# One row-by-row column in three groups instead of one in six: SyncE's share of the gather in a graph network's last edge pass

## The chip, the cores and the metric

One core of a Trainium2 chip runs the whole program in one launch. The metric is the device time of one execution in microseconds (us); the number compared is the median of several executions. The profile is one execution taken by the hardware profiler, with its own span.

The engines are called PE (TensorE), DVE (VectorE), ACT (ScalarE), POOL (GpSimd) and SP (SyncE). SP computes nothing: it waits, branches, loads registers and issues DMAs.

## The reference, cut to what matters

The reference is four graph layers on 12,500 nodes and 200,000 edges, sorted by destination. The change touches the last one, whose node features `h` have 64 floats:

```python
def _L3_gnn_ref(h, ef, gamma, beta, src, dst):
    z = h[src] + h[dst] + ef
    deg = segment_sum(ones, dst); deg_safe = maximum(deg, 1.0)[:, None]
    mean    = segment_sum(z, dst) / deg_safe
    mean_sq = segment_sum(z * z, dst) / deg_safe
    std = sqrt(relu(mean_sq - mean * mean) + EPS_STD)
    mx, mn = segment_max(z, dst), segment_min(z, dst)
    agg = concatenate([mean, mx, mn, std], axis=1)
    ...                        # degree scalers, mean over 13 parts, batch norm over the nodes
```

The edge pass computes, for every edge, the running sum and running maximum over its destination's edges of `h[src] + ef`, of its square and of its negative. The gather `h[src]`, one row of 256 bytes for each of the 200,000 edges, is what the change is about.

## The kernel before, in words

**Tiling.** The edges are padded to 128 x 1563 and laid out with partition p holding edges 1563p to 1563p+1562. A *group* is 16 edge columns (`GW`) of all 128 partitions; there are 98 (`NGRP`), the last one with 11 columns. A *column* is 128 edges, one on each partition, and to fetch it means to fetch 128 rows of `h_tab` from HBM. The fetched rows of a group go into one of six slots (`NY`) of the ring `y`: group g uses slot g % 6.

**Who fetches.** POOL fetches a column with one indirect DMA (L2305), 16 for a group. In slots that the list `taken` names, one column less: the last column (k = 15) of those groups comes from SP, through the class `SyncRows` (L303 to L345). SP does it row by row. It loads the 128 byte addresses of a column, prepared in HBM at the start of the program, into a small tile `at` (`load_places`, L314), waits until the slot is free (L323, L324), and then four times over loads 32 of the addresses into registers (L294, a TENSOR_LOAD) and issues 32 DMAs of one row each (L298). So a column of SP has four *quarters* of one TENSOR_LOAD and 32 row DMAs, and the two instructions of a row DMA are a MOVE and the DMA.

**Loops.** POOL's code is unrolled over all groups. SP's is a hardware loop, `with sp.Fori(1, NSYNC // 2 - 1) as n` (L335 onwards in `all_columns`), of one pass for every six groups, with the first and the last six groups written out before and behind it. `self.got` names the slots that SP serves, and the body has one column for each.

**The other edge passes.** The two transformer convolutions (`conv_edges`, gathers at L815) have SP fetch a column in slots 2 and 5, `SYNC_SLOTS = [2, 5]`, from the same table with the same class. The three attention passes (`gat_edges`, L1851) do too, and ACT fetches a third. Only the last pass, `pna_edges`, calls it with `single=True` and slot 5 alone.

**The chain of a group in the last pass.** DVE waits for the rows (POOL's and SP's, where the slot has both) and for the edge attributes that ACT has copied to PSUM, and adds them (L2334). This frees the slot (`added`): POOL waits on it before it fetches group g+6 (L2302), SP before it fetches the column of group g+6 (L324). ACT makes squares and negatives (L2440 to L2442), DVE runs five scans for the sums (L2349) and five for the maxima (L2355), ACT copies both to a row buffer (L2449, L2451) and issues the *store* of the group (L2454), 128 x 16 rows of 1 KB, 2048 KB in all. The last 11 columns are done as two pieces of 8 and 3. When all rows are stored, POOL gathers one row for each partition (L2310), and after a barrier the node stage begins (L2551 onwards).

The lines that decide what SP does:

```python
for b in range(max(self.first, self.single), 2):
    self.column(sp, 0, b, used)
with sp.Fori(1, NSYNC // 2 - 1) as n:
    for b in self.got:
        self.column(sp, n, b, used)
for b in self.got:
    self.column(sp, NSYNC // 2 - 1, b, used, b == 0)
```

Of the kernel before, what the change touches and what calls it, by code (L numbers as in the profile page):

```python
# [26 lines left out]
D = 64  # L27
# [28 lines left out]
SYNC_SLOTS, NSYNC = [EVERY - 1, NY - 1], NGRP // EVERY  # L56
# [170 lines left out]
def build(nc, a, out):  # L227
# [7 lines left out]
    def dram(name, shape, dt=F32):  # L235
        return nc.dram_tensor(name, shape, dt, kind="Internal").ap()
# [25 lines left out]
    h_tab = dram("h_tab", (NP_, D))  # L262
# [1999 lines left out]
    def pna_edges(tag, rows):  # L2262
# [3 lines left out]
        st = Stage(nc, tag, signals)  # L2266
        y, ea = st.sb("y", [P, NY, GW, D]), st.sb("ea", [P, 2, GW, D])
# [13 lines left out]
        ready = st.sem("edges_ready", 10)  # L2281
        mask_ready, lifted, added, row_ready = (st.piece_slots(n) for n in ("mask_ready", "lifted", "u_added", "row_ready"))
        e_loaded = st.dma_slots("e_loaded", 16 * HALF)
        taken = SYNC_SLOTS[1:]
        gathered, by_sync = st.pass_slots(taken), SyncRows(st, y, h_tab, D, 0, single=True)
        row_stored = st.store_slots("row_stored")
        squared, copied, summed, maxed = (st.sem(n, NPIECE) for n in ("squared", "u_copied", "summed", "maxed"))
        s_carried, m_carried = (st.sem(n, NPIECE - 1) for n in ("carried", "m_carried"))
# [404 lines left out]
    with ExitStack() as gat:  # L2693
# [14 lines left out]
        gat_to_pna("n5", rows_d[4], a["L2_gnn_b2"], gt)  # L2708

    pna_edges("c6", rows_d[5])  # L2710
    finish_pna("f6", rows_d[5])
    root.close()
# [39 lines left out]
```

## Time and profile before

| | us |
|---|---|
| median of 3 runs (13215.43 to 13219.89) | 13218.92 |
| the profiled execution | 13244.6 |
| its span, first to last instruction | 13242.9 |
| in it, POOL's gathers of the last edge pass (L2305), first to last start | 11095.8 to 13030.4 |

In the profile's page POOL is busy 74% of the span, DVE 51%, ACT 31%, PE 4%. The work of the five edge passes follows in time, so a share over the whole span says little: each pass is read by itself, from the first to the last instruction of its gather. A wait is read from the idle time in front of an instruction and from what ended it. SP never counts as busy; what it does is read from the timeline of its DMAs.

### The profile page before, as it was taken

To read this page: it belongs to the slowest core of one execution; us is meant where nothing else is said; L and a number is where in the kernel's file an instruction comes from. 1 tells how busy PE (TensorE), PEld (TensorE's weight loads), DVE (VectorE), ACT (ScalarE), POOL (GpSimd) and SP (SyncE) were. 2 spreads that over 40 slices of the span, in tenths; PEclk is the share of its full clock that TensorE was granted. 3 is DMA by queue.
4 is the path that set the end of the run, shared out by engine and by line. 5 is a ranking of instruction groups with operands and counts; after the bars stand their busy time and mean duration, and the time that the engine had idled before them with its cause. 6 is when DMAs were issued, how large, how long until landed. Compare 5 with 4: busy or idle time off the path is not lost. (4 is left out here: it accounts for less than half of the span.)

```text
span 13242.9 us, 103860 instructions
## 1 busy us (share of the span) xinstructions
PE 520.3 (4%) x1768; PEld 340.0 (3%) x1768; DVE 6799.1 (51%) x10545; ACT 4056.7 (31%) x3972; POOL 9825.8 (74%) x10362
## 2 busy tenths in 40 slices
PE   3000001100000300000010000000000000000001
PEld 1000000100000200000000000000000000000000
DVE  2777876377777533333333333343333336656656
ACT  4333333233333311111112111111111113666663
POOL 7777776777777677777777777777777776777775
PEclk9999999555555655555555555555555555555555
DMA  8445444344444222222212222222222223444443
GB/s 333 120 123 128 123 123 107 90 123 123 123 123 123 63 66 65 63 65 66 62 45 61 63 61 61 59 49 58 62 62 62 63 62 88 161 160 156 160 160 115
DMA packets 976807, 1317.32 MB, mean 99 GB/s; under 512 B 660843, under 2 KB 676674, under 8 KB 962815
## 3 DMA queue, kind: packets, MB, share of 16 engines
q10 hardware_dynamic: 557731, 803.76, 18.7%
q0 software_dynamic: 334400, 373.85, 14.8%
q1 hardware_dynamic: 83996, 134.02, 2.8%
q14 instruction: 666, 5.46, 0.1%
q8 instruction: 14, 0.23, 0.0%
HBM read 651.23 MB, written 659.53 MB: 99 GB/s over the span
## 5 line engine op out<-in xcount | busy, mean ns | idle before, releaser
L1851 POOL DMA_INDIRECT c_y<-g_tab,srcs x4545 | 4301.9, 947 | 1388.2 <-issue 1388.2
L2305 POOL DMA_INDIRECT c_y<-h_tab,srcs x1547 | 1463.9, 946 | 506.6 <-issue 471.7
L815 POOL DMA_INDIRECT c_y<-h_tab,srcs x1531 | 1448.2, 946 | 467.3 <-issue 467.3
L815 POOL DMA_INDIRECT first_y<-h_tab,srcs x1452 | 1373.5, 946 | 445.4 <-issue 442.9
L1883 DVE TENSOR_TENSOR c_s<-c_y,c_ad 128x64 f32<-128x64 f32 (+1 forms) x297 | 79.3, 267 | 1881.4 <-DMA c_y<-g_tab,srcs 1850.7
L1966 ACT ACTIVATE c_ex<-c_de 128x64 f32<-128x64 f32 (+1 forms) x297 | 67.4, 227 | 3171.8 <-issue 2852.7
L1919 DVE COPY c_w_in<-c_ex 128x64 f32<-128x64 f32 (+1 forms) x297 | 66.4, 224 | 1609.0 <-ACT c_ex L1966 1609.0
L1927 DVE TENSOR_TENSOR_SCAN c_acc<-c_r,c_w_in 128x1156 f32<-128x1156 f32 (+1 forms) x297 | 753.0, 2535 | 14.6
L837 DVE TENSOR_TENSOR_SCAN c_q_all<-c_mask,c_q_in 128x408 f32<-128x408 f32 (+2 forms) x792 | 733.7, 994 | 16.6 <-issue 9.1
L881 DVE TENSOR_TENSOR_SCAN c_acc<-c_r,c_w_in 128x408 f32<-128x408 f32 (+2 forms) x792 | 731.0, 986 | 8.2
L928 ACT ACTIVATE c_q_in<-c_q_raw 128x1552 f32<-128x1552 f32 (+1 forms) x198 | 596.6, 3013 | 280.9 <-DVE c_q_in L897 198.6
L1980 ACT ACTIVATE c_row<-c_acc 128x1088 f32<-128x1088 f32 (+1 forms) x297 | 617.8, 2080 | 0.0
L942 ACT ACTIVATE c_ex<-c_de 128x16 f32<-128x16 f32 (+1 forms) x198 | 37.1, 187 | 1784.2 <-DVE c_de L870 1784.2
L1920 DVE TENSOR_TENSOR c_w_in<-c_y,c_ex 128x1024 f32<-128x1024 f32 (+1 forms) x297 | 581.5, 1958 | 0.0
L956 ACT ACTIVATE c_row<-c_acc 128x1552 f32<-128x1552 f32 (+1 forms) x198 | 564.1, 2849 | 0.0
L2349 DVE TENSOR_TENSOR_SCAN c_acc_s<-c_mask,c_su 128x442 f32<-128x442 f32 (+2 forms) x495 | 477.6, 1031 | 128.9 <-ACT c_su L2440 128.8
L2334 DVE TENSOR_TENSOR c_su<-c_y,c_ea_ps 128x1024 f32<-128x1024 f32 (+1 forms) x99 | 185.5, 1874 | 652.7 <-DMA c_y<-h_tab,srcs 652.7
L2355 DVE TENSOR_TENSOR_SCAN c_acc_m<-c_penm,c_mu 128x442 f32<-128x442 f32 (+2 forms) x495 | 474.8, 1024 | 0.0
L1979 ACT ACTIVATE c_row<-c_fm 128x64 f32<-128x64 f32 (+1 forms) x297 | 91.5, 308 | 1139.0 <-DVE c_acc L1927 1139.0
L2449 ACT ACTIVATE c_row<-c_acc_s 128x2048 f32<-128x2048 f32 (+1 forms) x99 | 374.1, 3779 | 141.9 <-DVE c_acc_s L2349 137.6
L2451 ACT ACTIVATE c_row<-c_acc_m 128x2048 f32<-128x2048 f32 (+1 forms) x99 | 374.2, 3780 | 85.2 <-DVE c_acc_m L2355 85.2
L848 DVE TENSOR_TENSOR c_prod<-c_y,c_q_all 128x1552 f32<-128x1552 f32 (+1 forms) x99 | 173.2, 1749 | 366.2 <-DMA c_y<-h_tab,srcs 365.7
(405 smaller groups left out, 6429.7 us busy)
## 6 DMA issues: line engine op xcount, KB each, us to landing
rows_d<-c_row ACTq DMA_DIRECT2D x97, 2048.0 KB
c_y<-g_tab SPq DMA_DIRECT2D x12288, 0.3 KB
rows_d<-c_row ACTq DMA_DIRECT2D x291, 576.0 KB
rows_d<-c_row ACTq DMA_DIRECT2D x194, 784.0 KB
c_q_raw<-q_start ACTq DMA_DIRECT2D x194, 776.0 KB, 6.2
c_y<-h_tab SPq DMA_DIRECT2D x6144, 0.2 KB
c_y<-g_tab ACTq DMA_DIRECT2D x6144, 0.3 KB
q_start<-first_y SPq DMA_DIRECT2D x97, 776.0 KB, 8.8
```

The source lines that it names most:

```text
L815: nc.gpsimd.indirect_dma_start(y[:, g % NY, k, 0:D], None, h_tab, source(g, k))\
L837: last = v.tensor_tensor_scan(flat(qs[:, lo:hi]), flat(mk[:, 0:hi - lo]), flat(q_cur[:, lo:hi]), 0.0, ALU.mult, ALU.add)
L881: last = v.tensor_tensor_scan(flat(ac[:, lo:hi]), flat(rr[:, 0:hi - lo]), flat(w_cur[:, lo:hi]), 0.0, ALU.mult, ALU.add)
L928: act.activation(narrow(q_in[:, pc.b], pc.w)[:, :, 1:pc.w + 1], q_raw[:, pc.slot, pc.lo:pc.lo + pc.w].rearrange("p t f -> p f t"), ACT.Copy)
L956: act.activation(row[:, b, 0:w, 0:F], narrow(acc[:, b], w)[:, :, 1:w + 1].rearrange("p f t -> p t f"), ACT.Copy).then_inc(row_ready[b].h, 1)
L1851: nc.gpsimd.indirect_dma_start(y[:, g % NY, k, :], None, g_tab, source(g, k))\
L1920: v.tensor_tensor(w_heads[:, :, 0:JG, 1:w + 1], ys[:, :, 0:D].rearrange("p t (h j) -> p h j t", h=H), ex[:, :, 0:w].unsqueeze(2).to_broadc ...
L1927: v.tensor_tensor_scan(flat(ac), flat(rr), flat(w_cur), 0.0, ALU.mult, ALU.add).then_inc(summed.h, 1)
L1980: act.activation(row[:, b, 0:w, 0:F], narrow(acc[:, b], w)[:, :, 1:w + 1].rearrange("p f t -> p t f"), ACT.Copy).then_inc(row_ready[b].h, 1)
L2305: nc.gpsimd.indirect_dma_start(y[:, g % NY, k, :], None, h_tab, source(g, k))\
L2349: last = v.tensor_tensor_scan(flat(ac_s[:, lo:hi]), flat(mk[:, 0:hi - lo]), flat(su_c[:, lo:hi]), 0.0, ALU.mult, ALU.add)
L2355: last = v.tensor_tensor_scan(flat(ac_m[:, lo:hi]), flat(pm[:, 0:hi - lo]), flat(mu_c[:, lo:hi]), 0.0, ALU.add, ALU.max)
```

## The change

In `pna_edges` the list of the slots that have a column from SP grows from slot 5 to slots 2 and 5, and `SyncRows` is made without `single`.

```diff
-        taken = SYNC_SLOTS[1:]
-        gathered, by_sync = st.pass_slots(taken), SyncRows(st, y, h_tab, D, 0, single=True)
+        taken = SYNC_SLOTS
+        gathered, by_sync = st.pass_slots(taken), SyncRows(st, y, h_tab, D, 0)
```

POOL's program loses 16 indirect DMAs of the pass. The rows are POOL's around the last edge pass (L2305 is the gather, L2310 and L2312 the join behind it):

```order
 L2058 UNCONDITIONAL_BRANCH
 L2298 UNCONDITIONAL_BRANCH
-L2305 DMA c_y<-h_tab,srcs 128x64 x1547
+L2305 DMA c_y<-h_tab,srcs 128x64 x1531
 L2310 DMA c_got<-rows_d,fix_at 128x256
 L2312 DMA rows_d<-c_got,fix_at 200064x256
```

The columns that it no longer fetches are the last ones of groups 2, 8, ..., 92. On SP, these rows stand at what was the end of the loop's body (L294 is a register load of 32 addresses, L298 are row DMAs, L314 is the load of the next column's addresses, L323 the wait for the slot):

```order
 L294 TENSOR_LOAD c_at
 L298 DMA c_y<-h_tab 1x256 x32
-L314 ISA
-L314 DMA c_at<-places_d 1x128
+L319 ISA
+L314 ISA
+L314 DMA c_at<-places_d 1x128
+L323 REGISTER_ALU
+L294 TENSOR_LOAD c_at
+L298 DMA c_y<-h_tab 1x256 x32
```

Where the loop loaded the next addresses and branched back after four quarters, it now goes on with a second column of four quarters and branches after that; the addresses of the next column are loaded ahead of the rows of each.

The body has 256 row DMAs now, and had 128. One more column stands ahead of the loop and one more behind it. DVE has one more wait, for SP's column, ahead of the addition in slot 2 (L345); nothing of ACT and PE moves.

## Rows read from the trace of the kernel before

**Rows 1.** Waits of the last pass's stretch: us in total, times, longest us.

```profile
DVE c_su L2334 <- DMA c_y<-h_tab,srcs: 652.7, 97, 21.2
...
POOL c_y L2305 <- issue: 471.7, 1546, 0.3
```

**Rows 2.** The gathers of two passes: ns min/median/max, first and last start in us.

```profile
L2305 POOL DMA_INDIRECT c_y<-h_tab,srcs x1547: 941/947/1053, 11095.8 to 13030.4; - x194
```

```profile
L815 POOL DMA_INDIRECT c_y<-h_tab,srcs x1531: 941/947/1027, 2493.7 to 4408.0; - x192
```

**Rows 3.** SP's own waits in the last pass.

```profile
SPq L324 <- DVE c_su L2334: 812.3, 15, 64.4
```

**Rows 4.** Timeline of SP, last pass: start us, us, what.

```profile
11098.56 52.85 SPq L298 DMA_DIRECT2D c_y<-h_tab  x128
...
11580.48 58.30 SPq L298 DMA_DIRECT2D c_y<-h_tab  x128
11638.98 0.23 SPq L314 DMA_DIRECT2D c_at<-places_d  x1
...
12531.49 57.94 SPq L298 DMA_DIRECT2D c_y<-h_tab  x128
...
12887.73 58.86 SPq L298 DMA_DIRECT2D c_y<-h_tab  x128
```

**Rows 5.** The same, single quarters: one before the first store, two with one.

```profile
11098.56 10.36 SPq L298 DMA_DIRECT2D c_y<-h_tab  x32
```

```profile
11609.17 13.40 SPq L298 DMA_DIRECT2D c_y<-h_tab  x32
```

```profile
11624.84 13.94 SPq L298 DMA_DIRECT2D c_y<-h_tab  x32
```

**Rows 6.** SP's register loads without and with a store beside them (ns min/median/max).

```profile
L294 SPq TENSOR_LOAD <-c_at x2: 2123/2124/2126, 11109.0 to 11121.9; - x2
```

```profile
L294 SPq TENSOR_LOAD <-c_at x2: 5707/5726/5744, 11574.6 to 11590.7; - x2
```

**Rows 7.** SP's row DMAs of a quarter, without and with a store.

```profile
L298 SPq DMA_DIRECT2D c_y<-h_tab x32: 227/228/269, 11111.2 to 11121.6; - x32
```

```profile
L298 SPq DMA_DIRECT2D c_y<-h_tab x32: 224/225/1128, 11609.2 to 11622.3; - x32
```

**Rows 8.** Timeline of SP in the second convolution, two columns in the loop.

```profile
2777.83 52.95 SPq L298 DMA_DIRECT2D c_y<-h_tab  x128
2836.22 0.24 SPq L314 DMA_DIRECT2D c_at<-places_d  x1
2838.80 51.75 SPq L298 DMA_DIRECT2D c_y<-h_tab  x128
2890.87 0.22 SPq L314 DMA_DIRECT2D c_at<-places_d  x1
2893.35 50.91 SPq L298 DMA_DIRECT2D c_y<-h_tab  x128
2947.27 0.24 SPq L314 DMA_DIRECT2D c_at<-places_d  x1
2949.84 10.26 SPq L298 DMA_DIRECT2D c_y<-h_tab  x31
```

**Rows 9.** Queue of instruction fetches, 300 us of the second convolution, then of the last pass.

```profile
q14 instruction: 18, 0.15, 0.2%
```

```profile
q14 instruction: 2, 0.02, 0.0%
```

**Rows 10.** First convolution: SP's column and the DVE instruction that waited for it.

```profile
1783.45 52.77 SPq L298 DMA_DIRECT2D first_y<-h_tab  x128
...
1840.91 1.77 DVE L848 TENSOR_TENSOR c_prod<-first_y,c_q_all 128x1552 f32<-128x1552 f32 x1 [9.76 <-DMA first_y<-h_tab]
```

**Rows 11.** Timeline of the last pass's end: DVE's additions, scans, ACT's stores.

```profile
13016.07 0.35 ACTq L2454 DMA_DIRECT2D rows_d<-c_row  x1
...
13023.06 1.88 DVE L2334 TENSOR_TENSOR c_su<-c_y,c_ea_ps 128x1024 f32<-128x1024 f32 x1 [10.39 <-DMA c_y<-h_tab,srcs]
...
13026.19 4.88 DVE L2349 TENSOR_TENSOR_SCAN c_acc_s<-c_mask,c_su 128x442 f32<-128x442 f32 x5 [1.26 <-ACT c_su L2440]
...
13036.10 1.04 DVE L2334 TENSOR_TENSOR c_su<-c_y,c_ea_ps 128x512 f32<-128x512 f32 x1
...
13041.10 2.75 DVE L2349 TENSOR_TENSOR_SCAN c_acc_s<-c_mask,c_su 128x234 f32<-128x234 f32 x5
```

**Rows 12.** ACT's stores, from the page: those of this pass, those of the convolutions.

```profile
rows_d<-c_row ACTq DMA_DIRECT2D x97, 2048.0 KB
```

```profile
rows_d<-c_row ACTq DMA_DIRECT2D x194, 784.0 KB
```

## The prediction, made before the changed kernel had run

> **What bounds the kernel now.** I read the waits of the last pass first [rows 1]. POOL goes from gather to gather with never more than 0.3 us between two, 1546 times, and nothing else ends a gap in the pass: it never waits for a free slot. DVE has waited for gathered rows before 97 of its additions, 652.7 us in all, 6.7 us a group. So DVE and ACT have slack in every group and POOL's issue rate sets the pace. The second view is the gather itself [rows 2]: 1547 gathers from 11095.8 to 13030.4, (13030.4 - 11095.8) / 1546 = 1.2514 us each. The second convolution, with 1531 gathers and two columns in six groups on SP, needs 1914.3 us, the same 1.251 each. Six groups cost POOL 95 x 1.251 = 118.8 us now and 94 x 1.251 = 117.6 us after.
>
> The third view is SP's, because the change doubles its work. Now it waits 15 times for slot 5 to come free, 812.3 us in all, 54 us before each column [rows 3]. That is its whole reserve: of every 118.8 us it works about 64. Two columns take about 128 by that, and there are only 118.8. So the question of this change is what a column costs SP when it no longer waits.
>
> **POOL's part.** Removed: 16 gathers x 1.251 = 20.0 us, all of them on the path as long as POOL is the bound. Taken alone, that gives 20 us.
>
> **SP's part, a clean column.** Ahead of the first store of the pass a quarter has 32 row DMAs in 10.36 us [rows 5] and a register load of 2.12 us [rows 6]; with the small steps between, 12.5 us. Four make 50.0 us.
>
> **SP's part, the stores.** With a store of ACT issued in the quarter the same 32 DMAs take 13.40 or 13.94 us [rows 5], 3.0 or 3.6 more; single issues go from 0.225 to 1.13 us [rows 7]. Where a register load meets the start of a store, it takes 5.7 instead of 2.1 us [rows 6], 3.6 more. The mean of the four, 3.45 us, is what one store costs SP while SP is at work. It closes with the whole column: 58.30 us from first to last row DMA [rows 4] and 5.74 of the load ahead make 64.0, which is 50.0 + 14.0, and four stores fall into it, 3.5 each. Of the 15 columns of this pass that have stores throughout, the shortest I cite took 57.9 and the longest 58.9 us, while the first, nearly without stores, took 52.85 [rows 4].
> Each group has one store, so 95 of them (groups 0 to 94) are issued while SP works through its 32 columns: 95 x 3.45 = 328 us.
>
> **SP's part, between the columns.** In the second convolution, where the loop has two columns already, I take the time from the end of a column's last row DMA to the first of the next, with a register load of 2.1 us in it. Inside the body it is 2893.35 - (2838.80 + 51.75) = 2.8 us. Across the loop's branch it is 2949.84 - (2893.35 + 50.91) = 5.6 us in one round and 2838.80 - (2777.83 + 52.95) = 8.0 us in another [rows 8]. The one-column loop of the last pass issues its next address load 0.2 us behind its last row, 11638.98 against 11580.48 + 58.30 [rows 4], ahead of its branch, and has its long wait behind it, so it shows no price. So I take 2.8 - 2.1 = 0.7 us for each of the 31 steps between columns and 2.8 us more for each of the 13 branches back: 21.7 + 36.4 = 58 us. The dearer gap, 2.4 us more, I take for a fetch that met a store; that is in the 328 already.
> The Trainium skill, "Runtime: NRT & Kernel Launch", section "Instruction fetch mechanics", has the same: the instruction memory of such an engine holds 32 KiB, and a taken branch whose target has left it stalls for a DMA. By its figure of 64 bytes an instruction (its 16 KiB blocks are 256 instructions) my estimate is 17 KB for the body before and 34 KB for the body after. By this rule the branches cost something, as the rows have it, and the rival of the free branch below falls.
>
> **The sum.** SP's 32 columns: 32 x 50.0 + 328 + 58 = 1986 us, 124.1 for two columns. SP starts with two address loads instead of one, so at about 11096.7, and ends at 13082.7. From the last issue to DVE's start it was 4.7 us in one case of the first convolution, 1836.22 to 1840.91 [rows 10], a high one; I take 4. DVE then adds group 95 at 13086.7. Groups 96 and 97 have been gathered long before (POOL would be done at 13011), so DVE and ACT follow at their own pace. From the addition of 96 to that of 97 it is 13.0 us where ACT is idle, and the scans start 3.1 us behind the addition; where ACT still copies the group before, they start 5.0 us behind it, 1.9 more [rows 11]. So 97 is added 13.0 + 15.0 = 28 us behind 95, at 13114.7. Now it is added at 13036.10 [rows 11]. All that follows is the same chain, so the end moves by **+78.6 us**. POOL's 20 us do not come off: nobody waits for POOL in the end.
> Against the profiled execution that is 13242.9 + 79 = 13322 of span. The profiled execution was 26 us over the median of the runs; the shift carries over, and the forecast is 13218.9 + 78.6 = **13297 us**.
>
> **Small terms.** DVE's one wait more in slot 2 is an instruction in front of an addition that has 6.7 us of slack. Nothing is queued behind SP but its own columns until the barrier. For POOL, DVE would have to lag six groups before it found no slot; at the end it lags by some 106 us behind POOL's own rows of group 95 (11095.8 + 16 x 117.6 = 12977, and 4 to land), a good five groups, and even then POOL has its rows in before SP.
>
> **Bounds.** The cost of a store: 3.0 to 3.6 us, 95 times, -43 to +14 us on the shift; in the new rhythm stores should meet row DMAs more than register loads, which speaks for a little less than my 3.45, and the clean quarter may be 12.4 (-13 us). The branch back: from nothing (-36) to the dear gap each time, 13 x 2.4 more (+31). Landing: 1 us either way. All these fall together rarely.
>
> **Rivals.**
> *POOL stays the bound, faster.* SP's second column hides as it does in the second convolution, whose pass runs at POOL's pace, and 20 us come off: 13199 us. For it: the same class, table and slots there, at 2893.35 - 2777.83 = 115.5 us for two columns [rows 8]. Against it: its stores are 784 KB, these 2048 KB [rows 12]. It decides where 97 is added at 13036.1 again: SP must be done by 13036.1 - 28 - 4 = 13004, so 1907 us for 32 columns, 119.2 for two; I have 124.1. It would need stores at 2.6 us. The Trainium skill, "DMA: Bandwidth & Descriptors", section "Issuing engines are not separate DMA queues", calls the time to initiate a DMA "usually small relative to the DMA itself"; by that, the second column would be free and this rival would win. The rows say the opposite for rows of 256 bytes: the issuing is the whole 58 us.
> *The branch back costs nothing here*, since the fetch is done while SP is held up anyway: 36.4 us less, +42, 13261 us. For it: a round of 2.8 us more can be hidden behind the landing of a store's rows. Against it: 18 packets to 2 [rows 9].
> *Fetches and stores add up.* Each branch costs 2.4 us more, as the dear gap does, because the longer stores delay the fetch and the 3.45 does not contain it: +31, 13328 us.
>
> **How the numbers follow.** A measurement of this kernel can tell about 0.2%, 26 us, from no change. Chances: the forecast 0.63, the free branch 0.14, fetches and stores adding up 0.12, POOL still the bound 0.08, something else 0.03. The first lies over the bound almost wholly, the second for three quarters, the third wholly; the fourth is 20 us faster and so within the bound. Slower 0.83, same 0.15, faster 0.02. The range goes from 13240 (the free branch, with cheaper stores) to 13335; outside are POOL as the bound, half of the adding-up case and the tails.
>
> **What would show each step.** POOL's gathers: 1531, starting 1.251 us apart while it has slots. SP: no wait for DVE's addition left (812 us to nearly none); columns of 50 us and 10 us or so of stores each; 5.6 us or more instead of 2.8 between every second pair of columns; last row DMA near 13083. DVE: its long waits, some 30 us, before every third addition, put down to SP's rows, and none before the two between. If SP still waits for slots, or if its columns come at 58.8 us or faster, I am wrong. If it ends near 13046, the branch was free; if DVE or ACT turns out to be slower than 13 to 15 us a group, the end moves by that.

## The result, and the profile after

| | before | changed |
|---|---|---|
| median, us | 13218.92 (5 runs) | 13291.33 (5 runs, 13286.82 to 13292.63) |
| ratio | | 1.0055, interval 1.004 to 1.007 |
| span of the profiled execution | 13242.9 | 13285.1 |
| first gather of the last pass to DVE's addition of group 97 | 1940.3 | 2011.2 |

The change costs 72.4 us; 78.6 were forecast. The two profiled executions differ by 42 us only, because the last pass happened to begin 27.1 us earlier in the second one (11068.7 against 11095.8). So stretches inside the pass are compared from its own first gather: 70.9 us more to the addition of group 97, and from there to the end 206.8 us before and 205.2 after.

The waits of the changed kernel's last pass (us in total, times, longest us):

```profile
DVE c_su L2334 <- DMA c_y<-h_tab: 540.7, 31, 20.3
POOL c_y L2305 <- issue: 463.5, 1520, 0.3
...
DVE c_su L2334 <- DMA c_y<-h_tab,srcs: 64.6, 9, 21.2
```

DVE used to wait 97 times for POOL's rows (with `srcs` in the name) [rows 1]. Now it waits 31 times for the rows without `srcs`, SP's, and 9 times for POOL's. The wait that was 6.7 us before each group has become one of 17 us before each third. Of SP's own waits for DVE's addition, 812.3 us in [rows 3], no line is left in the pass: SP runs through. POOL does what was expected of it:

```profile
L2305 POOL DMA_INDIRECT c_y<-h_tab,srcs x1531: 938/944/1048, 11068.7 to 12985.1; - x192
```

1916.4 us for 1531 gathers, against 1934.6 for 1547 in [rows 2]. It ends 18.2 us earlier, and nothing comes of it. SP's timeline in the same pass, two columns in the loop body now (start us, us, what):

```profile
11379.16 57.66 SPq L298 DMA_DIRECT2D c_y<-h_tab  x128
11439.89 0.23 SPq L314 DMA_DIRECT2D c_at<-places_d  x1
11442.45 58.38 SPq L298 DMA_DIRECT2D c_y<-h_tab  x128
11501.14 0.23 SPq L314 DMA_DIRECT2D c_at<-places_d  x1
```

A column still takes 58 us from its first row DMA to its last [rows 4]; with the steps between, the 32 columns come 61.9 us apart (1981.1 / 32). Inside the body 0.3 us pass from the last row DMA to the next address load (11500.83 to 11501.14), across the branch 3.1 us (11436.82 to 11439.89); from row to row that makes 2.8 and 5.6, as in [rows 8]. The queue of instruction fetches, over 300 us of the pass:

```profile
q14 instruction: 17, 0.14, 0.1%
```

It had 2 packets in [rows 9]. Now the end of the pass:

```profile
12932.82 117.84 SPq L298 DMA_DIRECT2D c_y<-h_tab  x256
```

```profile
13051.62 1.88 DVE L2334 TENSOR_TENSOR c_su<-c_y,c_ea_ps 128x1024 f32<-128x1024 f32 x1 [15.26 <-DMA c_y<-h_tab]
...
13064.76 1.95 DVE L2334 TENSOR_TENSOR c_su<-c_y,c_ea_ps 128x1024 f32<-128x1024 f32 x1
...
13079.87 1.05 DVE L2334 TENSOR_TENSOR c_su<-c_y,c_ea_ps 128x512 f32<-128x512 f32 x1
```

SP's last row DMA ends at 13050.7. Group 95 is added 1.0 us later, 96 and 97 follow at 13.1 and 15.1 us without a wait, as the prediction took from [rows 11].

### The profile page after: what moved, and what is told of

Read it like the earlier page. It is cut to its first block and busy times, and to the rows that moved or that the text cites. A ratio compares the mean times of both kernels' runs of the same rounds, so it can differ in the third digit from the quotient of the medians.

```text
span 13285.1 us, 108106 instructions
## 1 busy us (share of the span) xinstructions
PE 516.0 (4%) x1768; PEld 339.2 (3%) x1768; DVE 6797.4 (51%) x10545; ACT 4057.1 (31%) x3972; POOL 9786.7 (74%) x10346
## 5 line engine op out<-in xcount | busy, mean ns | idle before, releaser
L2305 POOL DMA_INDIRECT c_y<-h_tab,srcs x1531 | 1445.5, 944 | 506.9 <-issue 463.5
```

Of the source, the lines that this page charges most:

```text
L2305: nc.gpsimd.indirect_dma_start(y[:, g % NY, k, :], None, h_tab, source(g, k))\
```

## The experiments

The theory: SP's time for its 32 columns sets the end; it is made of clean issuing (50 us a column), of 3.4 us for each store of ACT, and of the fetch at each branch back. The rivals: the fetch is hidden, POOL's pace still counts, or SP's rows slow the others on the DMA engines. The experiments are numbered in the order in which they ran. The changed kernel, timed again beside runs of the kernel before, gave the same difference.

### Experiment 11: the changed kernel again

> The changed kernel once more, beside the kernel before of these comparisons: 73 us over it. It gives the first experiment a partner that was timed against the same runs.

Measured: 13297.89 us against 13224.72, ratio 1.0055 (1.004 to 1.0071), 73.2 us. Differences to the kernel before, measured side by side, are what is compared below: +73 for the changed kernel.

### Experiment 1: the branch taken away

Shortened to what it does in the last pass (the other passes keep their loop):

```diff
-            with sp.Fori(1, NSYNC // 2 - 1) as n:
+            for n in range(1, NSYNC // 2 - 1):
                 for b in self.got:
                     self.column(sp, n, b, used)
```

> The changed kernel with SP's loop of the last pass written out: the same 32 columns in the same order, no branch back. My theory: the 13 branches cost 2.8 us each in fetched code, on top of the stores, so 36 us come off the changed kernel's 13291, to 13255; SP's time from first register load to last row DMA falls from 1981 to about 1945 us. Rival (the fetch is hidden behind the stores anyway, or written-out code is fetched as slowly): no change, 13291.

Measured: 13266.27 us against 13214.53, ratio 1.0039 (1.0024 to 1.0054), +51.7. So 21.5 us came off, not 36. SP's timeline:

```profile
11562.91 58.78 SPq L298 DMA_DIRECT2D c_y<-h_tab  x128
11621.74 0.24 SPq L315 DMA_DIRECT2D c_at<-places_d  x1
11624.24 58.73 SPq L298 DMA_DIRECT2D c_y<-h_tab  x128
11683.02 0.24 SPq L315 DMA_DIRECT2D c_at<-places_d  x1
```

The gaps are gone: 0.05 us from a row DMA to the next address load, and 2.5 us from row to row each time. Summed over the pass, the 31 gaps fell from 125.8 to 82.6 us, 43 us. But the columns grew, 58.7 us where the changed kernel has 58.0, over 32 of them from 1853 to 1873 us. The number of stores in that time is 95 in both. What grew shows in the row DMAs of the two runs (ns min/median/max), the changed kernel's first:

```profile
L298 SPq DMA_DIRECT2D c_y<-h_tab x3077: 224/225/1149, 11560.0 to 13050.4; - x193
```

```profile
L298 SPq DMA_DIRECT2D c_y<-h_tab x3072: 227/228/1230, 11562.9 to 13030.7; - x192
```

The median row DMA, one that no store disturbs, takes 228 ns in the written-out code and 225 in the loop. Over 4096 of them 3 ns are about 12 us of the 20 (an estimate; the first two columns are at 228 in both). The rest, about 8 us, is 0.1 us more for each store: measured against each run's own median, a store cost 3.4 us in the changed kernel and 3.5 here. So the branch costs what the rows said, 43 us over all steps between columns, and the written-out code loses half of that again inside the columns. Why its row DMAs take 3 ns more is not settled by these runs.

### Experiments 2 and 5: the bytes of the stores halved

```diff
-   act.dma_start(by_edge(rows)[:, bass.ds(pc.col, w), :], row[:, b, 0:w]) ...
+   act.dma_start(by_edge(rows)[:, bass.ds(pc.col, w), :], row[:, b, 0:w, 0:F]) ...   # rows of 2 * D floats
```

> The changed kernel, but of each row of the last pass's result only the half with the sums is stored (512 bytes instead of 1 KB, 1024 KB a group, as many rows), and the node stage and the join read that half twice; the maxima are computed and copied but not used. My theory: a store holds SP up for as long as its bytes take, so a store costs about 1.7 instead of 3.4 us, SP needs about 1820 us for its columns, POOL is the bound again: 13199, a few us less for the smaller last stores. Rival (the number of row descriptors decides, or the hold-up is not the stores' at all): 13291.

Measured: 13190.70 us against 13214.53, ratio 0.9982 (0.9973 to 0.9991), 24 us faster than the kernel before. Its waits:

```profile
DVE c_su L2334 <- DMA c_y<-h_tab,srcs: 515.0, 77, 21.1
...
DVE c_su L2334 <- DMA c_y<-h_tab: 116.4, 20, 11.2
```

DVE waits for POOL again. As many rows are stored, each with half the bytes, and SP gets through its 32 columns in 1876 us instead of 1981. That is less of a gain than the 1820 expected: summed over SP's rows, the time lost in row DMAs (what each took over the median of 225 ns) fell by half, from 310 to 158 us, but the register loads took 326 instead of 280 us. A store costs SP about 2.3 us here and 3.4 with all bytes. With a third less of it the 16 gathers come off.

The edit changes more than the bytes. The queue of ACT's DMAs over the same 300 us, in the changed kernel and here (packets, MB, share of the 16 engines):

```profile
q10 hardware_dynamic: 4195, 37.28, 32.6%
```

```profile
q10 hardware_dynamic: 34256, 24.18, 27.5%
```

So bytes fell to half and packets rose sixteenfold, and SP lost a third less: the count of packets is not what holds SP up in the full store. How much of the remaining 2.3 us comes from the many small packets, and so whether the bytes alone would count in proportion, these runs can't tell.

The same on the kernel before, as the control:

> The kernel before with the same half of the rows stored (the maxima are computed and not used). It tells how much of the second experiment's gain is the change of SP's time and how much comes with smaller stores anyway. My theory: POOL's 1547 gathers are the bound either way, 13219, less 2 to 6 us for the last stores and landings. Rival (the stores hold the whole pass up): 30 us or more under 13219.

Measured: 13211.12 us against 13217.04, ratio 0.9996 (0.9986 to 1.0006), 6 us less and within the interval. So of the 24 us some 18 belong to the change of SP's share: the 16 gathers, nearly whole. In the two traces, the time from the first gather to the addition of group 97 is 1914.4 and 1934.1 us, 19.7 apart.

### Experiment 3: POOL's gathers put back

```diff
+   if g % NY == SYNC_SLOTS[0] and g < NGRP - NY + SYNC_SLOTS[0]:
+       nc.gpsimd.indirect_dma_start(spare[:, g // NY, :], None, h_tab, source(g, SYNC_K)).then_inc(spare_got.h, 16)
...
+   pool.wait_ge(*spare_got(16 * (NSYNC // 2)))
```

> The changed kernel, with POOL still fetching its 16 columns, now into a spare tile that nobody reads. My theory: nobody waits for POOL in the end, so its 16 x 1.251 us cost nothing: 13291, within 5 us. Rival (POOL's pace still counts, since it has nearly run out of slots, and the change's true cost is 20 us more): 13311.

Measured: 13294.30 us against 13214.53, ratio 1.0059 (1.0044 to 1.0075), +79.8 where the changed kernel has +73. The two intervals, some 20 us to either side, are too wide to tell 7 from 20; the traces can. From the first gather to the addition of group 97 it is 2012.3 us here, 2011.2 in the changed kernel and 2012.7 in its repetition, and SP needs 1982.2 us for its columns, against 1981.1 and 1982.2. So POOL's 16 gathers cost about 1 us at most within the pass: in the changed kernel POOL's pace does not count.

### Experiments 6 and 8: the size of the loop's body

```diff
                 part(lo, SYNC_SLOTS[b], self.got[b])
+            if self.single and not isinstance(n, int):
+                spare = row_reader(sp, mybir.EngineType.SP, self.at[b:b + 1, :], self.spare, 0, self.tab, self.width)
+                for q in range(2):
+                    spare(NREG * q, 0, self.spare_got)
```

> The kernel before, where SP's loop body fetches two more quarters (64 rows) into a spare tile that nobody reads: six quarters in the body, where there were four, and eight in the changed kernel. SP still has a reserve of some 15 us a round, so the time stays at 13219. My theory: what is paid at the branch is the fetch of a body that has grown too large, so with six quarters the instruction queue shows few packets still (2 to 6 in 300 us) and the next register load starts under 1 us behind the branch when no slot is waited for; if the limit lies lower than I think, it has 12 packets or more. Rival (the second column's own structure or its address load causes the gap): no fetches whatever the size.

Measured: 13215.67 us against 13217.04, ratio 0.9999 (0.9988 to 1.0009): no change, since SP still waits for its slot, 15 times and 395.1 us in all. The queue of fetches, over the same 300 us as above:

```profile
q14 instruction: 16, 0.13, 0.1%
```

And one of its branches back, with the next instruction behind it:

```profile
L340 SPq COMPARE_BRANCH  x1: 50/50/50, 11407.9 to 11407.9; - x1
L340 SPq FUSED_REGOPS  x1: 65/65/65, 11410.7 to 11410.7; - x1
```

So a body of six quarters is fetched every round just like one of eight, and its 13 branches each show a pause of 2.4 to 2.8 us, as those of the changed kernel do; in the kernel before it is 0.3 us (11401.2 to 11401.5). Here the pause costs nothing, because it falls into SP's wait for the slot. What brings the pause is the size, not the second column as such, and the limit lies lower than I thought, between four quarters and six.

With `range(4)` in place of `range(2)`:

> The kernel before, where SP's loop body fetches four more quarters into a spare tile: the changed kernel's work for SP, but DVE waits for SP once in six groups only, and POOL keeps its gathers. SP has 30 columns' worth: 1500 + 12 + 49 + 328 = about 1890 us, with 11 us more if branches are dearer. My theory: the last column comes at about 1890 to 1900 us, just under what decides: 13219 to 13225, and the instruction queue shows 15 to 20 packets in 300 us. Rival (SP's rows on the DMA engines slow the others): 13240 or more.

Measured: 13247.36 us against 13217.04, ratio 1.0022 (1.0012 to 1.0033), +30 where 0 to 6 were expected. SP's own waits in the pass tell what I had left out:

```profile
SPq L324 <- DVE c_su L2340: 64.2, 1, 64.2
```

With one slot SP cannot run ahead: its second column waits 64 us for slot 5, once, and the estimate of 1890 us had no wait in it. 1890 + 64 would be 1954; the trace has 1939. The three or so stores that fall into that wait (64 / 19.6) cost SP nothing, which is 11 us of the 15 by an estimate at 3.4 us each. That SP's rows slow the others is not it: POOL's 1547 gathers took 11071.8 to 13002.9, 1931.1 us, no more than in [rows 2].

This run also shows the dear gap of [rows 8]. Of its 13 branches back, two come 2.0 and 1.1 us after the issue of a store, and the next instruction follows after 6.1 and 6.3 us. The second of them (the store was issued at 11945.3):

```profile
L340 SPq COMPARE_BRANCH  x1: 45/45/45, 11946.4 to 11946.4; - x1
L340 SPq FUSED_REGOPS  x1: 65/65/65, 11952.6 to 11952.6; - x1
```

Ten of the others took 2.4 to 2.7 us, and one 3.6. So a fetch that meets a store is some 3.6 us longer, about what a store costs SP in its rows. The columns behind these two branches take 58.7 and 59.0 us, hardly more than the others.

### Experiments 4, 7, 9 and 10: SP with fewer columns

POOL keeps slot 2's column in the last two rounds, of 0 to 15 (SP's code is written out here and in the next ones). The line on POOL's side:

```diff
-   for k in range(by_pool(g, taken)):
+   for k in range(by_pool(g, taken) + (g % NY == SYNC_SLOTS[0] and g // NY in range(kept, NSYNC // 2))):   # kept = 14
```

> SP serves slots 2 and 5 as in the changed kernel, but in the last two of 16 rounds slot 2 is left to POOL, and SP's columns are written out. So SP has 30 columns: 30 x 50 + 20 + 95 x 3.4 = 1843 us, under the 1907 that decide. My theory: POOL is the bound again, with 14 gathers less: 13219 - 14 x 1.251 = 13201. Rival (the load on the DMA engines by SP's rows slows the rest): 13219 or more.

Measured: 13207.09 us against 13214.53, ratio 0.9995 (0.9986 to 1.0004), 7 us faster, which the interval does not tell from no change, where 17.5 were expected. The next run shows why.

In the last round only:

> As the fourth experiment, with slot 2 left to POOL in the last round alone: 31 columns, 31 x 50 + 21 + 328 = 1899 us, just under the 1907 that decide. My theory: 13219 - 15 x 1.251 = 13200, up to 13210 if SP ends a little late. Rival: as for the fourth.

Measured: 13238.26 us against 13217.04, ratio 1.0017 (1.0007 to 1.0026), 21 us slower, a clear miss. SP was on time: its last column was out 1898 us after the first gather, as computed. DVE was not. Its additions from the last long wait on, in that run's timeline:

```profile
12910.81 1.88 DVE L2361 TENSOR_TENSOR c_su<-c_y,c_ea_ps 128x1024 f32<-128x1024 f32 x1 [17.13 <-DMA c_y<-h_tab]
12923.95 1.94 DVE L2361 TENSOR_TENSOR c_su<-c_y,c_ea_ps 128x1024 f32<-128x1024 f32 x1
12939.34 1.91 DVE L2361 TENSOR_TENSOR c_su<-c_y,c_ea_ps 128x1024 f32<-128x1024 f32 x1
12954.56 1.94 DVE L2361 TENSOR_TENSOR c_su<-c_y,c_ea_ps 128x1024 f32<-128x1024 f32 x1
...
13030.94 1.04 DVE L2361 TENSOR_TENSOR c_su<-c_y,c_ea_ps 128x512 f32<-128x512 f32 x1
```

No wait for data stands before any of the eight additions behind the first. After the first step of 13.1 us they follow each other at 15.3 us, which is DVE's and ACT's own pace when both have work. POOL's is 19.6. So a lag that SP has caused is made up at 4 us a group, and what is not made up when the pass ends stays. That SP is on time with its last column is not enough. The fourth experiment ends the same way: its last 12 additions up to that of group 97 (12829.8 to 12998.2) stand 15.3 us apart without a wait for rows, so it too was still catching up when the pass ended.

The test is to give the same relief, spread over the pass:

> As the fourth experiment, but the rounds in which POOL keeps slot 2's column are spread: rounds 4, 9 and 14 of 0 to 15. In the fourth, SP fell some 70 us behind POOL over 14 rounds, and DVE and ACT could make up only 4 us a group of it (15.3 against 19.6 us). Spread, the lag should stay under 25 us and be made up each time: POOL is the bound, with 13 gathers less: 13217 - 13 x 1.251 = 13201. Rival (what the fourth lost was not the catching up but SP's load on the DMA engines): 13207 or more.

Measured (`left = 4, 9, 14`): 13204.30 us against 13224.72, ratio 0.9985 (0.9976 to 0.9994), 20 us faster than the kernel before.

> The same with POOL keeping slot 2's column in rounds 5 and 12: 14 gathers less, but the last three rounds build up 15 us of lag again. Theory: 13217 - 17.5 + some 5 for the end = 13204. Rival: as for the ninth.

Measured (`left = 5, 12`): 13207.19 us against 13224.72, ratio 0.9987 (0.9978 to 0.9996), 17.5 us faster. The difference between the two is 2.9 us, and the expectations have 3.8; both came out 4 to 5 us faster than expected, within their intervals. The waits of DVE in the run with three:

```profile
DVE c_su L2360 <- DMA c_y<-h_tab,srcs: 511.4, 80, 21.2
...
DVE c_su L2360 <- DMA c_y<-h_tab: 93.6, 7, 17.2
```

DVE waits for POOL's rows 80 times and for SP's 7 times: POOL sets the pace again, with 13 gathers less. This version beats both kernels, by 0.15% against the one before.

## Why the prediction was right

The direction, the mechanism and the size held; 13297 us were forecast and 13291.33 measured. Step by step, times from the pass's first gather:

- **SP becomes the bound.** Shown by DVE's waits, by SP's missing ones, and by the third experiment, in which POOL's gathers cost about 1 us at most. The columns come 61.9 us apart; at 58.8 they would have hidden.
- **SP's time.** Forecast 1986 us, measured 1981.1. In it the stores: 3.45 us forecast, 3.40 measured, 95 of them in both. That the stores hold SP up, and not through the number of their packets, is shown by the second experiment; that it goes by their bytes alone is not. The clean column of 50.0 us was taken ahead of the loop, where a row DMA takes 228 ns; in the loop it is 225 [rows 7]. So 128 clean rows take about 0.4 us less there, and the stores' part of a column is larger by as much. The sum hardly feels it, since the two were fitted together to a whole column.
- **The branch back.** Forecast 2.8 us dearer, 13 times; in the trace 5.6 against 2.8 us each time. That the dear gap of [rows 8] was a fetch that met a store was right, as the eighth experiment shows. That none of the 13 in this pass was dear is partly luck, for the forecast did not work it out: DVE's additions wait for SP's rows, so ACT's stores follow SP's columns in a fixed rhythm, and every branch back comes 9.7 to 12.3 us behind a store's issue and 17 us or more ahead of the next. In the second experiment, where POOL sets the pace, that distance drifts over the pass, and two branches, each 0.4 us behind a store, take 3.7 us. The expectation of the first experiment, "36 us come off", failed: 21.5 came off, because the written-out code issues each row DMA 3 ns slower and a store costs 0.1 us more in it. The rival of the free branch is out. That of fetches and stores adding up did not occur in this rhythm; the eighth experiment, where a met fetch cost no more than the store would have in the rows, speaks against it.
- **Landing.** Forecast 4 us, measured 1.0 (13050.66 to 13051.62). Next to the 4.9 us of SP's time this is the other error of the sum, and the largest for its size; the row of the first convolution [rows 10] was no good stand-in. The last store before it had been issued at 13039.9, 10.7 us ahead of the last row, and its packets were out by then.
- **The end.** 28 us from the addition of 95 to that of 97 forecast, 28.3 measured. 78.6 - 4.9 - 3.0 + 0.2 = 70.9, the measured shift inside the pass.
- **DVE's waits** were forecast at some 30 us before each third addition and were 17. The 30 is the distance between two additions there (32 to 35 us), of which DVE works 13 to 15; I had written the one for the other.
- **POOL** waited for slots 10 times, 8.4 us in all, where I had seen it just short of that.
- **Where POOL as the bound begins.** The point that I gave, SP done by 1907 us, is wrong in general. It takes DVE for caught up. With 31 columns SP was done at 1898, and the pass was 16 us longer than before all the same. Nothing in the forecast hung on it, since SP was far beyond.

## What to carry to other kernels

When a queue that has been waiting gets more work, count its waits as its reserve, and cost a unit of its work by what it takes under the load of exactly that stage: the same class cost 115.5 us for two columns in one pass and 124 in another, and 117.6 was the limit. A loop body that grows can come to be fetched anew in every round, and the trace shows it in the fetch queue's packets before any time is lost. A helper that is a little too slow need not be dropped: relieve it now and then over the whole stretch, not at the end, because the lag is paid back only as fast as the consumers can run ahead of the producer.

## What the runs showed of the hardware that was not expected

- Half the bytes in sixteen times as many packets (2048 of 512 bytes for 128 of 16,384) took a third off what a store costs SP, 2.3 instead of 3.4 us. The row DMAs lost half as much, the register loads more than before (326 against 280 us in the pass).
- A loop body of 398 instructions (six quarters) is fetched again each round, with 16 packets in 300 us, like one of 534 (17), while one of 268 is not (2). The instructions are counted in the trace from branch to branch.
- Written-out code took 12 packets in those 300 us and showed no gap; only the branch back showed the fetch, as a pause of 2.4 to 2.8 us, and of 6.1 and 6.3 us where a store had been issued 1 to 2 us before.
- The same row DMA takes 228 ns (median) in the written-out code of the first experiment and 225 in the loop. These runs don't say why.
